# Gate matmul of chunk 0 ahead of the probabilities' transposes, and Gelu in the order 0, 1, 2, in the two feed-forward stages

## What is computed

```python
def _layer(x, wqkv, qs, ksc, wo, lg, lb, w1, b1, w2, b2):
    h = shift_token(x)
    q, k, v = jnp.split(h @ wqkv, 3, axis=-1)          # 8 heads of 64
    q = l2norm(q) * qs; k = l2norm(k) * ksc            # then rotary_xpos(q, k)
    o = local_attention(q, k, v)                       # windows of 64, each sees itself and the one before
    x = x + o @ wo
    h = shift_token(x)
    h = (h - mu) / jnp.sqrt(var + 1e-05) * lg + lb
    a, g = jnp.split(h @ w1 + b1, 2, axis=-1)          # 341 columns each
    x = x + (a * gelu(g)) @ w2 + b2
    return x
```

## Time and profile before

| | |
|---|---|
| Median of 3 runs | 2177.14 us (2174.58 to 2178.0) |
| The profiled execution: its own time | 2163.13 us |
| The profiled execution: span, first to last instruction | 2161.4 us |
| Mean granted TensorE clock, share of full | 0.977 |
| TensorE matmul (PE) busy | 1991.7 us, 92% |
| VectorE (DVE) busy | 1773.1 us, 82% |
| ScalarE (ACT) busy | 1369.1 us, 63% |
| GpSimd (POOL) busy | 1233.1 us, 57% |

### The profile page before, as it was taken

The page is one execution under the profiler, slowest core; times in us unless marked ns, Lnnn a source line. Parts: engine busy times, 40 slices in busy tenths (PEclk is TensorE's granted clock), DMA queues, the critical chain, the costliest instruction groups (busy, mean ns, idle before and its releaser), DMA issues. The chain is left out here.

```text
span 2161.4 us, 45576 instructions
## 1 busy us (share of the span) xinstructions
PE 1991.7 (92%) x16998; PEld 1090.6 (50%) x16998; DVE 1773.1 (82%) x2383; ACT 1369.1 (63%) x3435; POOL 1233.1 (57%) x599
## 2 busy tenths in 40 slices
PE   6687899999999999789999999967999999999997
PEld 2233555555555555345444444434555555555553
DVE  6986798998999997458888888547998998999983
ACT  8454566667667666336676766745666667666663
POOL 0217777777877775434122222257777777777760
PEclk9799999999999999999999999989999999999999
DMA  2004111211111210242322222022211111111111
GB/s 64 0 1 119 43 36 36 47 38 36 45 39 32 46 36 21 71 121 66 90 51 51 51 51 51 15 82 64 49 37 36 45 40 31 45 41 35 41 31 44
DMA packets 85473, 101.38 MB, mean 47 GB/s; under 512 B 13504, under 2 KB 60552, under 8 KB 83208
## 3 DMA queue, kind: packets, MB, share of 16 engines
q1 hardware_dynamic: 82824, 96.77, 17.9%
q10 hardware_dynamic: 2432, 1.70, 0.3%
HBM read 33.94 MB, written 10.49 MB: 21 GB/s over the span
## 5 line engine op out<-in xcount | busy, mean ns | idle before, releaser
L848 POOL TENSOR_TENSOR ffn_RN<-ffn_SS,ffn_mhalf 128x16 f32<-128x16 f32 x128 | 372.5, 2910 | 274.2 <-DVE ffn_SS L794 273.8
L842 POOL TENSOR_TENSOR ffn_QK<-ffn_T 128x1024 f32<-128x1024 f32 x128 | 420.2, 3283 | 18.3 <-DVE ffn_T L742 18.1
L2004 DVE TENSOR_REDUCE attn_b_NX<-attn_b_s 128x1 f32<-128x512 f32 (+3 forms) x608 | 368.9, 657 | 74.9 <-PE attn_b_s L1696 69.8
L589 ACT ACTIVATE ffn_PB<-ffn_s,ffn_NM 128x128 f32<-128x128 f32 x1024 | 360.6, 390 | 101.0 <-DVE ffn_NM L764 101.0
L1922 ACT ACTIVATE attn_b_PT<-attn_b_s 128x1024 f32<-128x1024 f32 (+1 forms) x320 | 286.9, 943 | 131.9 <-PE attn_b_s L1730 131.6
L633 ACT ACTIVATE ffn_SQ<-ffn_w 128x1024 f32<-128x1024 f32 x128 | 131.1, 1024 | 308.0 <-DVE ffn_T L742 307.7
L836 POOL TENSOR_TENSOR ffn_PB<-ffn_PB,ffn_RDEN 128x1024 f32<-128x1024 f32 x128 | 243.7, 1904 | 25.9 <-DVE ffn_RDEN L727 25.9
L378 PE MATMUL ffn_w<-ffn_Wqkv,ffn_H 128*128 128x512 f32 x512 | 244.5, 600 | 9.2 <-ACT ffn_SQ L633 5.6
L589 ACT ACTIVATION_READ_ACCUMULATOR ffn_PB<-ffn_s,ffn_NM 128x1 f32 x1024 | 236.5, 231 | 0.0
L1696 PE MATMUL attn_b_s<-attn_b_KS,attn_b_QS 62*128 62x512 f32 (+3 forms) x768 | 231.8, 402 | 0.0
L758 DVE TENSOR_TENSOR ffn_QK<-ffn_QK,ffn_RN 128x1024 f32<-128x1024 f32 x128 | 221.4, 1730 | 0.4 <-POOL ffn_RN L848 0.3
(11 more groups left out here) (250 smaller groups left out, 3760.5 us busy)
## 6 DMA issues: line engine op xcount, KB each, us to landing
ffn_Voff<-ffn_Vcur SPq DMA_DIRECT2D x248, 128.0 KB, 2.3
ffn_H<-ffn_Y SPq DMA_DIRECT2D x64, 128.0 KB, 2.5
ffn_H<-ffn_U SPq DMA_DIRECT2D x64, 128.0 KB, 2.5
attn_b_QS<-attn_b_qk_parts SPq DMA_DIRECT2D x64, 128.0 KB
attn_b_KS<-attn_b_qk_parts SPq DMA_DIRECT2D x64, 128.0 KB
attn_b_qk_parts<-attn_b_RP SPq DMA_DIRECT2D x6, 1024.0 KB, 9.7
ffn_rope<-in_ffn_rope_dram SPq DMA_DIRECT2D x4, 1024.0 KB, 8.0
attn_b_rope<-attn_b_OS SPq DMA_DIRECT2D x252, 16.0 KB
```

The costliest lines, as they stand in the source:

```text
L589: last = act.activation(PB[:, x % 2, e, p, :], s_ps[:, e, p * P:(p + 1) * P], ACT.Exp, bias=NM[:, x % 2, e, p:p + 1], accum_out=DEN[:, x % ...
L842: pool.tensor_tensor(QK[:, x % 2, :, :, :].rearrange("p c q k -> p (c q k)"), T1[:, :, :, :].rearrange("p c h k -> p (c h k)"), T2[:, :, : ...
L848: pool.tensor_tensor(RN[:, x % 2, :], SS[:, x % 2, :], mhalf[:, :], ALU.pow).then_inc(rnorm, 1)
L2004: dve.tensor_reduce(at, bank, AX_X, ALU.max, negate=True).then_inc(s1_read, 1)
```

## The change

Three things change inside `ffn_stage`. TensorE's gate matmul of chunk 0 moves from behind gate 1 to ahead of `turn_probs`, and needs only `hn` there; gate 1 stays behind `turn_probs` with its wait for `ynext`. ScalarE's Gelus go in the order of chunks 0, 1, 2. The waits that count Gelus follow: gate 2 now needs the first Gelu of its group and value 2 the second, where it was the other way round, and `hide` counts for chunks 0 and 1 are exchanged. The last group keeps both gates behind the transposes, in the order 0, 1.

```diff
-                    pe.wait_ge(gelu, 3 * g + 2)
+                    pe.wait_ge(gelu, 3 * g + 1)
                     hidden(g, 1, 2)
...
-                    pe.wait_ge(gelu, 3 * g + 1)
+                    pe.wait_ge(gelu, 3 * g + 2)
                     hidden(g, 0, 2)
-                if real(i - 1):
-                    turn_probs(i - 1)
-                g = mlp_at(i, "gate10")
+                g = mlp_at(i, "gate01")
                 if g is not None:
                     pe.wait_ge(hn, g + 1)
                     if g % NT == 0:
                         pe.wait_ge(s_w1, g // NT + 1)
+                    if g < LAST:
+                        hidden(g, 1, 0)
+                if real(i - 1):
+                    turn_probs(i - 1)
+                if g is not None:
...
                     elif g >= 1:
                         pe.wait_ge(ynext, g)
+                    if g == LAST:
+                        hidden(g, 1, 0)
                     hidden(g, 1, 1)
-                    hidden(g, 1, 0)
...
-                    for n, j in enumerate((1, 0, 2)):
+                    for n, j in enumerate((0, 1, 2)):
...
-                dve.wait_ge(gelu, 3 * g + {1: 1, 0: 2, 2: 3}[j])
+                dve.wait_ge(gelu, 3 * g + {0: 1, 1: 2, 2: 3}[j])
```

More of the change, by code:

```diff
@@ L232, in mlp_at @@
             ahead = {"gate2": (0, 2), "value2": (0, 2), "value1": (1, 2), "value0": (1, 2), "wo": (1, 1),
-                     "centre": (2, 1), "mean": (2, 1), "w2": (3, 2), "gate10": (3, 1)}
+                     "centre": (2, 1), "mean": (2, 1), "w2": (3, 2), "gate01": (3, 1)}
             at, lag = ahead[phase]
```

## The result

The changed kernel takes 2160.3 us in the median of 5 executions (2156.8 to 2164.4), the kernel before in the same comparison 2174.6 (2167.8 to 2178.0): a ratio of 0.9942, with a 95% interval of 0.9917 to 0.9968, or 14.3 us less (7 to 18). Repeated with more executions: 2160.3 against 2172.3, ratio 0.9951 (0.9932 to 0.9970). The direction is the forecast one. The profiled execution of the changed kernel is the longest of its five, 2164.4 us with a span of 2162.7, so the two profiled spans (2161.4 before) say nothing of the gain. Nor do those of the repetition: 2170.8 for the changed kernel, again the longest of its executions, and 2168.5 before. Stretches have to be compared.

What follows compares the result with a forecast made beforehand. TensorE was taken as the bound, with matmuls busy for 92% of the span. Per stage 2.8 - 0.35 + 0.58 + 0.5 = 3.5 us, 7.1 for two: 2177.1 - 7.1 = 2170.0 us, range 2165 to 2177.

Steps and rivals of the forecast that it cites:

- The stall: Step 3, first layer: gate 1 waits for VectorE's L773 on bank 1; covering this brings TensorE 0.35 us sooner.
- The price: First layer: transposed probabilities ready 0.86 us later, so GpSimd's division and L758 end 0.86 late; exponentials still 0.22 sooner.
- The gain in the first layer: Groups 1 to 8: the 0.35 us a group survives whole, by a hair; 2.8 us a stage.
- The gain from the new order of the Gelus is nothing here: First layer, groups 1 to 8: gate 2 waited for the second Gelu at most 0.16 us; taken as zero.
- The second layer: Groups 9 to 13: exponentials 0.4 us late, mostly absorbed in step 1; net loss 0.35 us a stage.
- I take a net loss of 0.07 a group: Second layer, groups 9 to 13: 5 x 0.07 = 0.35 us a stage, between a gain of 0.35 and a loss of 0.28 each.
- The ends of a stage: Gate 2 needs an earlier Gelu: 0.58 us gained in group 0, 0.5 in group 14; both together 0 to 1.2.
- The sum: Both feed-forward stages: 3.5 us gained in each, 7.1 us in two; chance 0.50.
- The time: Whole kernel: 2177.1 - 7.1 = 2170.0 us, 0.33% less, carrying over the 14 us between profiled execution and median.
- the rivals: Four alternatives: gain in both layers (0.15), gain eaten in the first too (0.15), slower (0.10), L758 ahead of GpSimd's division (0.10).
- full gain: Rival: the second layer gains 0.35 us a group too, 11.3 us in all, 2165.9 us; chance 0.15.

Runs made afterwards that it cites:

- the late addition: The changed kernel with the second layer's addition into X moved from ahead of the sums of squares to the end of VectorE's step: 2157.16 us, ratio 0.9933.
- one fill: The changed kernel with one idle VectorE fill of 1.2 us between the last addition to X and the third stage: 2162.38 us, ratio 0.9971.

## Why the prediction was right in direction and wrong in size

**The stall, right.** Gate 1 no longer waits: 1.16 us became 0.87, the block 2.94 became 2.59. L777 ends at 523.99, 0.6 us ahead of gate 1 (0.7 forecast).

**The price, right.** L840 starts 0.24 earlier than L836 did, while everything of TensorE comes 1.44 earlier in this execution (526.35 against 527.79), so it is 1.20 later against the projection behind it; forecast 0.86 later against a block that itself comes 0.35 sooner, 1.21. L762 takes 2.71 us (forecast 2.4 to 2.7), ends 1.08 behind the division, and the exponentials start at the end of the maxima.

**The gain in the first layer, right in kind, a little small.** Forecast 0.35 a group, measured 0.42: 0.39 in step 3 and 0.03 in step 0, the Gelu order's. The stall itself was taken too small, from a group where the block took 2.94 us; in most it takes 3.00, and 2.59 after the change (0.02 less than this shows in the length of step 3).

**"The gain from the new order of the Gelus is nothing here", wrong.** Alone it is worth 0.16 a group; beside the move only 0.03 of it is left. The prediction took 0.16 as the upper bound of gate 2's wait and chose zero; the wait was 0.09. That the two figures of 0.16 agree is chance, as the 0.16 by itself is 0.07 of step 3 and 0.09 of step 0.

**The second layer, wrong in mechanism.** The forecast was a loss of 0.07 a group, from exponentials 0.4 late. Measured is 0.18, through the copy of k. I had followed VectorE's delayed queue to L743, L762 and what hangs on these, and passed over the copy of k, which frees the bank that `attend` writes. In the first layer it costs 0.07 too, and as TensorE keeps this lateness unchanged from L448 to the end of the step, the exponentials added nothing to it there. The step that failed is "I take a net loss of 0.07 a group", for want of that wait. The exponentials start 699.48 - 690.74 = 8.74 us behind L378 in the second layer and 534.48 - 526.35 = 8.13 in the first; the difference is the 0.6 that `attend` lost, and they cost nothing of their own, as the group of 40.94 with the late addition shows.

**The ends of a stage, right.** Group 0 gained 0.57 (0.58 forecast), groups 14 and 15 together about 0.9 (0.5), a mean of values that spread more than it. Gate 2 of group 0 now waits 1.15 us, and not 1.72, in the view of weight loads:

```profile
283.28 0.27 PEld L453 LDWEIGHTS ffn_m<-ffn_HN,ffn_W 128*114 128x114 f32 x2 [1.15 <-ACT ffn_G L621]
```

**The sum, 7.1 us for the stages, right within 0.5**, with 7.6 measured, in part by luck: the larger stall, the Gelus and the ends offset the second layer's loss of 0.18 a group where 0.07 was forecast.

**The time, wrong.** The step that failed is the first sentence, "The change touches only the two feed-forward stages, so I read those", together with the carrying over of the sum to a median of three. The instructions that change are only there, but the time of the third stage isn't fixed: it has two lengths 10 us apart, with the granted clock, and the median depends on how the executions fall. The sum lacked that term, 4 to 7 us in these medians; that the shares account for all of it is the best reading of the runs and not proof. The forecast was 2170.0 and the measured time 2160.3: of these 9.7 us, 7.2 are the difference between the kernels (14.3 for 7.1), and 2.5 are the median of before itself, 2177.1 in three executions and 2174.6 in the five of the comparison. The profiled execution of before was itself at the short end (a span of 2161.4 at 0.977), and the 14 us between it and the median of the runs, which I carried over, was the sign of it. None of the rivals had this mechanism: full gain, the nearest in time at 2165.9, did not happen.

## What to carry to other kernels

When a move makes another engine's work late, go through that engine's queue instruction by instruction and name who first waits for each; the price was paid by a copy that looked like mere filling. Where a wait can be covered by work of the same kind that is already beside it, reorder within the pair and leave the others in place: transposes first, then gate 0 and gate 1, beats both kernels: its groups take 40.87 us in both layers, and without the third stage it stands 15.0 us under the kernel before. And where a profiled execution lies many times the expected gain from the median, ask which stage differs between executions before adding a few microseconds to either.

## What the runs showed of the hardware

**A stage can have two lengths.** The third stage took 546 us where the 30 us from 926 to 956 were granted 0.94 of the clock, and 556 where they were granted 0.60, with the same instructions. Idling 3.6 us ahead of it raised the medians by 8.6 and 8.5 us and left none of 24 executions at a mean clock of 0.974 or more.

**The start of the second feed-forward stage, too.** Its first L378, four instructions, took 1.98 us in the profile of before and 3.42 in that of the changed kernel:

```profile
1434.76 3.42 PE L378 MATMUL ffn_w<-ffn_Wqkv,ffn_H 128*128 128x512 f32 x4 [1.34 <-DMA ffn_H<-ffn_Y]
```

The first two groups of this stage took 84.8 and 82.2 us in two profiles of before, 88.1 and 86.0 in two of the changed one; in these executions this takes back some of the 7.6. It isn't the change's doing: the changed kernel with one fill took 82.2. In the 13 profiles the two groups took 82.2 to 85.0 us where their granted clock was 0.92 to 0.94, and 85.5 to 88.1 where it was 0.88 to 0.90, whatever the kernel.

**A wait can be hidden by its label.** The weight load of L448 in the second layer is said to have idled for "issue", though it waited for the copy of k; only the row of the matmul names the releaser:

```profile
693.20 0.23 PEld L448 LDWEIGHTS ffn_w<-ffn_PT,ffn_Voff 128*64 128x64 f32 x4 [1.40 <-issue]
```

In the first layer the same label stands for 0.80 us, and the difference, 0.60, is what the second layer loses against the first. In the kernel before, where L448 starts 1.81 us behind L378, it stands for 0.76.
